# A two-layer graph network: record positions found in two parts, checks put behind the normalisation, casts split four to three

## What is computed

```python
h = relu(layernorm(x))
msg = w[:, None] * ((h @ W_i)[dst] + (h @ W_j)[src] + edge_attr @ W_e)
x = x + segment_sum(msg, dst) + h @ W_self
h = relu(layernorm(x))
def sage(h, Wl, b, Wr):
    return (segment_sum(h[src], dst) / max(count, 1)) @ Wl.T + b + h @ Wr.T
x = x + log_softmax(sage(relu(sage(h, W1l, b1, W1r)), W2l, b2, W2r))
```

## Time and profile before

| what | value |
|---|---|
| median of three runs | 1537.78 us |
| the profiled execution, its own time | 1539.19 us |
| its span | 1536.8 us |
| PE, weight load, DVE, ACT, POOL busy, share of the span | 80%, 64%, 68%, 46%, 70% |
| chain that ended last | POOL 27%, issue 10%, PE 5%, DMA 1% |
| mean granted clock of TensorE | 0.945 of full speed |
| queue of software gathers | 33552 packets, 69.34 MB |

### The profile page before, as it was taken

The page is one execution under the profiler, slowest core; times in us unless marked ns, Lnnn a source line. Parts: engine busy times, 40 slices in busy tenths (PEclk is TensorE's granted clock), DMA queues, the critical chain, the costliest instruction groups (busy, mean ns, idle before and its releaser), DMA issues. The chain is left out here.

```text
span 1536.8 us, 27420 instructions
## 1 busy us (share of the span) xinstructions
PE 1222.6 (80%) x9615; PEld 990.7 (64%) x9615; DVE 1048.8 (68%) x2116; ACT 713.3 (46%) x1202; POOL 1071.2 (70%) x1044
## 2 busy tenths in 40 slices
PE   0157888888898898888875489888989888879887
PEld 0146677677787677767653277667777666667665
DVE  7776777987888788877786255545554655656565
ACT  3323544654565546554675143433333444434344
POOL 4777777777777777776777547777773077777770
PEclk9998999999999999999999699999999999999998
DMA  7478545665666556644577457656665755665663
GB/s 241 112 174 251 156 142 172 196 193 149 191 205 183 162 157 193 193 136 121 190 224 241 112 161 197 167 170 174 173 175 144 191 171 162 178 189 164 181 172 87
DMA packets 320509, 266.98 MB, mean 174 GB/s; under 512 B 32329, under 2 KB 297956, under 8 KB 320372
## 3 DMA queue, kind: packets, MB, share of 16 engines
q1 hardware_dynamic: 272708, 189.44, 42.1%
q0 software_dynamic: 33552, 69.34, 17.1%
q10 hardware_dynamic: 14112, 6.43, 1.5%
HBM read 212.08 MB, written 53.00 MB: 172 GB/s over the span
## 5 line engine op out<-in xcount | busy, mean ns | idle before, releaser
L852 POOL DMA_INDIRECT Dt<-h_d,idx x624 | 626.2, 1004 | 199.0 <-issue 189.6
L1458 POOL DMA_INDIRECT Dg<-g_d,idx x390 | 418.7, 1074 | 205.7 <-issue 148.2
L1419 PE MATMUL pc<-Kt,hi 128*128 128x512 f32 (+1 forms) x980 | 400.4, 412 | 14.5 <-issue 5.8
L1419 PE MATMUL pc<-Kt,lo 128*128 128x512 f32 (+1 forms) x980 | 382.4, 394 | 0.0
L1352 DVE CAST Kt<-Ut 128x2048 fp32r<-128x2048 uint8 (+3 forms) x168 | 234.4, 1402 | 53.1 <-PE pc L1419 44.1
L1247 ACT ACTIVATE Cb<-pc 128x784 uint8<-128x784 f32 x304 | 240.2, 823 | 50.9 <-PE pc L1235 48.6
L1419 PEld LDWEIGHTS pc<-Kt,hi 128*128 128x128 f32 x980 | 192.4, 196 | 57.9 <-issue 17.0
L1419 PEld LDWEIGHTS pc<-Kt,lo 128*128 128x128 f32 x980 | 191.9, 196 | 34.6
L1354 ACT ACTIVATE Kt<-Ut 128x1536 fp32r<-128x1536 uint8 (+3 forms) x112 | 181.6, 1623 | 64.4 <-PE pc L1419 55.8
L1209 DVE TENSOR_TENSOR Jt<-ps,keyT 128x1568 bf16<-128x1568 bf16 x204 | 196.5, 969 | 4.5 <-PE pc L1235 1.7
L1235 PE MATMUL pc<-Jt,Rt 128*128 128x196 bf16 x1216 | 148.4, 252 | 42.6 <-ACT Cb L1247 33.9
(11 more groups left out here) (155 smaller groups left out, 1545.9 us busy)
## 6 DMA issues: line engine op xcount, KB each, us to landing
Ut<-c_d SPq DMA_DIRECT2D x126, 448.0 KB
Dt<-in_ea SPq DMA_DIRECT2D x208, 192.0 KB
c_d<-Cb SPq DMA_DIRECT2D x38, 784.0 KB
Dq<-in_ea SPq DMA_DIRECT2D x77, 192.0 KB
Dt<-h_d,idx POOLq DMA_INDIRECT x624
g_d<-ht ACTq DMA_DIRECT2D x98, 64.0 KB
r_d<-rt SPq DMA_DIRECT2D x98, 64.0 KB
sp<-g_d SPq DMA_DIRECT2D x14, 448.0 KB, 4.8
```

Of the source, the lines that this page charges most:

```text
L852: e.indirect_dma_start(Dt[:, s, t, 0:128], None, h_d, bass.IndirectOffsetOnAxis(idx[:, c:c + 1], 0))\
L1419: last = e.matmul(pc[:, k % 2, 0:n], part[:, q, :], Kt[:, t % NK, j - q0, 0:n], start=(x == 0 and t % 2 == 0 and j == 0 and part is hi), s ...
L1458: e.indirect_dma_start(Dg[:, s, t, :], None, (g1_d, g2_d)[L], bass.IndirectOffsetOnAxis(idx[:, c:c + 1], 0)).then_inc(s_gg[s], 16)
```

## The change

1. **Start.** `chk` is loaded in two pieces: the 234 columns that the window starts need go first, the 1671 columns of the checks after the seven parts of `H`. The checks (L381 to L390) and the copy of the flag run on DVE behind the last `scale`. The positions are found in two parts, windows 0 to 6 after `scale(2)` and 7 to 12 after `scale(4)`, each once its own gathers have landed, and POOL starts its window gathers with the first part.
2. **Node counts.** They are a task of their own behind `flip_weights`, with their store; `flip_counts` moves from group 1 to group 3.
3. **Weights in PSUM.** For four octets at a time DVE copies the three parts of the weights from `wp` to a corner of PSUM bank 3 (`wpp`), and the multiplications read them there. `give_r` of layer 1 moves from bank 3 to bank 2.
4. **Block normalisation.** The step that adds epsilon to the variance (L1061) goes; ACT adds it as a bias of the root, and the three Newton steps are written in another form, as many as before.
5. **Casts.** `unit_by` was: two units in five on ACT, whatever their size. Now every unit of four row blocks is on ACT, every unit of three on DVE.

```diff
+PARTS = ((0, 7), (7, NWC))
 LAG = {
-    "count.pe": 1, "load_group.sp": 5, "load_group.dve": 1,
+    "count.pe": 1, "load_group.sp": 5, "load_group.dve": 1, "flip_weights.dve": 1, "node_counts.dve": 1,
+    "node_counts.sp": 5,
 }
+        epst = sb("epst", [128, 1], F32)
+        wpp = ps[3][:, :].bitcast(BF16)[:, 512:704].rearrange("p (a w two) -> p a w two", w=32, two=2)
         def common_sp(e):
-            e.dma_start(chk[:, :], A["chk"]).then_inc(s_ld, 16)
+            e.dma_start(chk[:, KC:NCHK], A["chk"][:, KC:NCHK]).then_inc(s_ld, 16)
...
+            e.dma_start(chk[:, 0:KC], A["chk"][:, 0:KC]).then_inc(s_lk, 16)
...
+            def positions(part):
+                k0, k1 = PARTS[part]
+                n = k1 - k0
+                e.wait_ge(s_rf[part], 16 * n)
+                link(e, e.tensor_tensor(rcm[:, k0:k1, :], rows[:, k0:k1, :],
+                                        thr[:, k0:k1].unsqueeze(2).broadcast_to([128, n, 128]), ALU.is_lt))
+                link(e, e.tensor_reduce(cnt[:, k0:k1], rcm[:, k0:k1, :], AX.X, ALU.add))
...
             stats(0)
             for c in range(7):
                 if c + 1 < 7:
                     stats(c + 1)
-                if c == 1:
-                    e.wait_ge(s_vp, 1)
-                    e.tensor_copy(flag[0:1, 0:1], ps[2][0:1, 0:1]).then_inc(s_flag, 1)
                 scale(c)
-                if c == 2:
-                    e.wait_ge(s_rf, 16 * NWC)
...
+                if c in (2, 4):
+                    positions((c - 2) // 2)
+            checks()
+            e.wait_ge(s_vp, 1)
+            e.tensor_copy(flag[0:1, 0:1], ps[2][0:1, 0:1]).then_inc(s_flag, 1)
...
             for k in range(KW):
+                if k == PARTS[0][0]:
+                    e.wait_ge(s_pos, 1)
+                if k == PARTS[1][0]:
+                    e.wait_ge(s_pos, 2)
...
             e.sem_inc(s_tab, 1)
+
+        def node_counts(e):
             here = rows[:, :, :].bitcast(F32)
...
-            def shifted(e):
-                e.wait_ge(s_t3, n + 1)
                 if n >= 2:
                     e.wait_ge(s_q2, n - 1)
-                e.tensor_scalar(ve[:, i, 0:1], mv[:, i, 0, 1:2], EPS, None, ALU.add).then_inc(s_x1, 1)
+                e.bn_aggr(mv[:, i, 0, :], st[:, i, 0, :]).then_inc(s_x1, 1)
...
-                e.activation(sd[:, i, 0:1], ve[:, i, 0:1], ACT.Sqrt).then_inc(s_q2, 1)
+                e.activation(sd[:, i, 0:1], mv[:, i, 0, 1:2], ACT.Sqrt, bias=epst[:, 0:1]).then_inc(s_q2, 1)
...
-            o = (0, 3)[L]
+            o = (0, 2)[L]
...
+                    if m % 4 == 0:
+                        pair = wp[:, :, 8 * m:8 * m + 32, :].rearrange("p a w two -> p a (w two)").bitcast(F32)
+                        link(e, e.tensor_copy(ps[3][:, 256:352].rearrange("p (a w) -> p a w", w=32), pair))
                     for part, to in ((1, RW[:, m % 2, 0, :, :]), (2, RW[:, m % 2, 1, :, :]), (0, own)):
-                        e.tensor_tensor(pairs(to), pairs(own), each(wp[:, part, 8 * m:8 * m + 8, :], 64), ALU.mult)
+                        e.tensor_tensor(pairs(to), pairs(own), each(wpp[:, part, 8 * (m % 4):8 * (m % 4) + 8, :], 64), ALU.mult)
...
-        unit_by = ["act" if t % 5 in (1, 3) else "dve" for t in range(4 * NI)]
+        unit_by = [("act", "dve")[t % 2] for t in range(4 * NI)]
...
-        task("take_group", dve=windows, sp=cnt_out)
+        task("take_group", dve=windows)
...
         flip_weights()
+        task("node_counts", dve=node_counts, sp=cnt_out)
...
-                if g == 1 and u == 1:
+                if g == 3 and u == 1:
                     flip_counts()
```

More of the change, by code:

```diff
@@ L318, in build @@
         s_ld = sem("s_ld")
+        s_lk = sem("s_lk")
         s_li = sem("s_li")
@@ L322, in build @@
         s_c1 = sem("s_c1")
-        s_rf = sem("s_rf")
+        s_rf = [sem(f"s_rf{i}") for i in range(2)]
         s_pos = sem("s_pos")
@@ L380, in common_dve, with checks @@
             e.tensor_tensor(wv[:, 13:26], cnt[:, :], con[:, CC2:CC2 + NWC], ALU.is_gt)
[L381 to L390, removed]
+            def checks():
+                e.wait_ge(s_lk, 16)
+                e.scalar_tensor_tensor(wv[:, 26:29], chk[:, KL:KL + 3], -31.0, chk[:, KF:KF + 3], ALU.add, ALU.is_gt)
+                e.tensor_tensor(wv[:, 29:30], chk[:, KG:KG + 1], con[:, CLB:CLB + 1], ALU.is_lt)
+                e.tensor_tensor(wv[:, 30:31], chk[:, KH:KH + 1], con[:, CUB:CUB + 1], ALU.is_gt)
+                link(e, e.tensor_tensor(ck1[:, 0:831], chk[:, KA:KA + 831], chk[:, KA + 1:KA + 832], ALU.is_gt))
+                e.tensor_reduce(wv[:, 31:32], ck1[:, 0:831], AX.X, ALU.add)
+                e.tensor_scalar(ck2[:, 0:831], chk[:, KA:KA + 831], 2, None, ALU.arith_shift_right)
+                link(e, e.tensor_scalar(ck3[:, 0:831], chk[:, KB:KB + 831], 2, None, ALU.arith_shift_right))
+                link(e, e.tensor_tensor(ck1[:, 0:831], ck2[:, 0:831], ck3[:, 0:831], ALU.is_equal))
+                link(e, e.tensor_reduce(wv[:, 32:33], ck1[:, 0:831], AX.X, ALU.add))
+                e.tensor_reduce(vt[:, :], wv[:, 0:33], AX.X, ALU.add).then_inc(s_v, 1)
             def stats(c):
@@ L414, in scale @@
                     .then_inc(s_rs, 1)
+            def positions(part):
[5 more added lines that the diff above has]
+                link(e, e.tensor_reduce(cnt[:, k0:k1], rcm[:, k0:k1, :], AX.X, ALU.add))
+                link(e, e.scalar_tensor_tensor(c1f[:, k0:k1], c1f[:, k0:k1], 128.0, cnt[:, k0:k1], ALU.mult, ALU.add))
+                if part == 0:
+                    e.tensor_scalar(pos[:, k0:k1], c1f[:, k0:k1], 2.0, None, ALU.mult).then_inc(s_pos, 1)
+                else:
+                    e.tensor_scalar(pos[:, k0:KW], c1f[:, k0:KW], 2.0, None, ALU.mult)
+                    e.tensor_scalar(pos[:, KW:NWC], c1f[:, KW:NWC], 3.0, None, ALU.mult).then_inc(s_pos, 1)
             stats(0)
@@ L456, in common_pool @@
             e.wait_ge(s_c1, 1)
[L457 to L460, removed]
+            for part, (k0, k1) in enumerate(PARTS):
+                for k in range(k0, k1):
+                    e.indirect_dma_start(rows[:, k, :], None, A["dsr"], bass.IndirectOffsetOnAxis(c1i[:, k:k + 1], 0))\
+                        .then_inc(s_rf[part], 16)
             for k in range(KW):
+                if k == PARTS[0][0]:
+                    e.wait_ge(s_pos, 1)
+                if k == PARTS[1][0]:
+                    e.wait_ge(s_pos, 2)
                 e.indirect_dma_start(win[:, k, :], None, A["rec"], bass.IndirectOffsetOnAxis(pos[:, k:k + 1], 0))\
@@ L689, in build @@
                              "s_qe", "s_mm")]
-        s_t1, s_t2, s_t3, s_t4, s_t5, s_t6, s_t7 = [sem(f"s_t{i}") for i in range(1, 8)]
+        s_t1, s_t2, s_t4, s_t5, s_t6, s_t7 = [sem(f"s_t{i}") for i in (1, 2, 4, 5, 6, 7)]
         s_h, s_pt, s_pv, s_pr, s_pq = [sem(n) for n in ("s_h", "s_pt", "s_pv", "s_pr", "s_pq")]
@@ L1070, in act @@
                     e.wait_ge(s_r2, n - 1)
-                e.activation(sd[:, i, 0:1], ve[:, i, 0:1], ACT.Sqrt).then_inc(s_q2, 1)
-            task("block_mix", pe=pe, dve=[product, add, moments, variance, shifted], sp=[sp], act=[act])
+                if n == 0:
+                    e.wait_ge(s_ep, 1)
+                e.activation(sd[:, i, 0:1], mv[:, i, 0, 1:2], ACT.Sqrt, bias=epst[:, 0:1]).then_inc(s_q2, 1)
+            task("block_mix", pe=pe, dve=[product, add, moments, variance], sp=[sp], act=[act])
         def block_norm(b):
```

27 lines of the change are left out of this document (12 added, 15 removed).

## The result

The changed kernel takes 1499.99 us (median of 4 runs, 1498.96 to 1503.49), the kernel before 1538.59 beside it (4 runs, 1536.27 to 1540.11): a ratio of 0.9754, 95% interval 0.9733 to 0.9776. Run again later beside 11 runs of the kernel before at 1540.02, it took 1499.72, ratio 0.9733 [0.9691, 0.9776]. The profiled execution has a span of 1497.0 us, where it was 1536.8.

A forecast was written before the change was run, and what follows sets the result against it. POOL's gathers bound stage 2, PE with DVE mostly stage 1. Start and node counts +2, DVE -2, stage 1's end -1, layers -18 and -19, ACT +4: -34 us off the median 1537.8, forecast 1504, range 1491 to 1523.

The forecast's parts named there:

- What bounds which stage: Stage 2 is bound by POOL; stage 1 by PE with DVE, and by POOL only from 703 us to its end.
- The casts: Stage 2: no casts of 2048 on DVE saves POOL 40 us; -18 in layer 0, -19 in layer 1 reach the end.
- ACT, +4: Stage 2: ACT's large casts sometimes come late for PE, costing 4 us, bounds 0 and 31.
- The start: Before stage 1's gathers: POOL's first gather at 47 to 50 us, DVE's first step at 45.5 to 48.5, first `Jt` +3.
- +2, -2 and -1 for stage 1: Start and node counts +2 us, DVE in the middle of stage 1 -2, end of stage 1 -1.
- (c): Stage 1 bound by POOL, or start's gain passes through: another 8 to 20 us, 1485 to 1497; chance 0.09.
- (d): Stage 2: DVE's three-row-block casts hold POOL too, or the delay has another source: 1537 to 1541 us; chance 0.04.
- (a): ACT becomes stage 2's limit; if half the gain, 17 us, is eaten, 1521 us; chance 0.12.
- (b): Stage 2: ACT's casts so late that the kernel is slower, 1544 us at 0.35 us each; chance 0.03.

The follow-up runs named there:

- casts alone: The kernel before with only the casts split four to three between ACT and DVE: 1504.51 us, ratio 0.9759 to the kernel before.
- four outer: The changed kernel with DVE's casts written over four column parts as outer dimension instead of three row blocks: 1546.28 us, ratio 1.0038 to the kernel before.
- mixed split: The changed kernel with the old split of casts for each layer's first nine and last thirteen units: 1493.24 us, ratio 0.9706 to the kernel before.
- the repeat: The changed kernel run again unaltered, beside a kernel before of 1540 us: 1499.72 us, ratio 0.9733.

## Why the prediction was right, step by step

**What bounds which stage.** Right. Stage 2 follows POOL: 44 us less of gathers brought 35.5 (casts alone), 52.6 us more cost 46.6 (four outer). Stage 1 does not: 16 us more of POOL in it moved the time by -0.9.

**The casts.** Right in mechanism, too small in size. I charged 40 us of POOL and 37 at the end of the layers; the gathers lost 45.5, and from the first gather to PE's last full group the layers are 20.9 and 23.3 us shorter where I had 18 and 19. My count of the kernel before had put gathers that touch a cast of each size with the rest. By any overlap, 67 met casts of 2048 alone and lost 39.2 us against 0.945 each, and 17 met both sizes and lost 7.4 more; both losses went. Gathers that meet no cast took 0.952 us before and 0.956 after.

**ACT, +4.** The term was mis-sized, and I had it at another place: late ACT casts spread over the layer. PE's waits for ACT's casts came to 2.4 us at the start of the stage and 1.7 in layer 1, and two waits for DVE's casts in the middle of layer 1 to 7.3. The loss shows in the stage at its seams, 5.3 us ahead of its first gather and 6.2 behind its last. The mixed split gave back 4.4 of the first and 4.1 of the second (against the repeat). At the end the cause was not ACT's load alone, as four outer shows, but the order of DVE's slow casts and ACT's behind them. The 3.5 us that the mixed split leaves there are PE behind POOL: it starts its last full gather group 1.7 us after POOL's last gather, where it started 2.2 us ahead of it before the change. Two misses cancelled: inside the layers POOL's part became 45.1 us shorter where I had 37, and the seams cost 11.5 where I had 4. That the time came out 4 us from the forecast is in part luck.

**The start.** The forecast of 47 to 50 us for POOL's first gather failed: 44.12. I had bounded it by POOL's branch behind the flag at DVE's price of 4.46 us; the row says that it waited for `h_d`. DVE's 45.95 lay within its 45.5 to 48.5. The first `Jt` was 0.8 us later, not 3, since the weights came 4.2 us earlier. None of it matters at the end: +2, -2 and -1 for stage 1 stand against -3.1, and -2.5 in the repeat.

**The rivals.** (c) fell by the run with the weights in SBUF. (d) fell by the gathers beside the slow casts, and by four outer, which is that rival built: 1546 where I had worked out 1537 to 1541. (a) and (b) did not come: PE's waits for ACT's casts stayed at 4.1 us. The page VectorE: DVE Perf Modes of the Trainium skill (section Mode 2x_2P) grants the two-port mode to an even outermost dimension, or to an odd one that is equal on both sides. I had read the trace wrongly against this page. The source code writes three row blocks on both sides, but in a full unit the three rows of the destination touch, and the trace records the cast with three rows at the source and one run of 1536 elements at the destination. Three and 1536 are neither both even nor equal, so by the page such a cast is slow, and it took 1745 ns. Four outer is recorded with four on both sides and took 972 ns. The 14 short casts of 768 elements are recorded with three on both sides; they took 701 ns on average, and at the slow rate half the elements would have taken at least half of 1745 ns, 873 (an estimate). The trace agrees with the page in all three, and the page was no ground for (d). The forecast did not suffer, because it went by the measured durations.

## What to carry to other kernels

Where POOL issues gathers on the bound path, read each gather beside what DVE does at that moment: a fast DVE instruction can be the dearer one. Look for the same element count at two speeds, and choose the slow order where DVE has slack. Judge the shape of an access by the pattern that the trace records, not by the source, since rows that touch were recorded here as one run. And before taking load off an engine, ask whether somebody waits for it in that stage: 44 us off stage 2's gathers brought 35.5 of 40.3 us, 19 us off stage 1's only made POOL wait.

## What the runs showed of the hardware that was not expected

The first is the price of an order of visit: 972 or 1746 ns for one and the same cast of 128 x 1536 from uint8 to fp32r, written with four or three as its outer dimension, and on average 1.40 against 0.95 us for the gather beside it.

The second is open. Beside a kernel before of 2132 us the variant with four outer took 2170.43 us, later 1546.28. Its waits in both (PE's weight loads first, total, times, longest):

```profile
PEld pc L1263 <- issue: 249.2, 153, 11.5
POOL Dt L877 <- PE ps L902: 537.6, 46, 23.8
```

```profile
PEld pc L1263 <- issue: 54.4, 106, 1.2
```

Casts and gathers last as long in both (975 and 972 ns; 970 and 973 ns in stage 1), and the DMA queue with most of the traffic was busy for the same time (29.4% of 2179.8 and 41.5% of 1547.7 us, 641 and 642 us). What differs is, first, TensorE's mean granted clock, 0.81 against 0.94; PE was busy for 1397 us instead of 1230. Second, there are pauses of more than 5 us for which the profile names no instruction as releaser: 31 ahead of weight loads, 55 on DVE and 45 on ACT, against one each in the later run. PE's longer busy time accounts for 167 of the 632 us at most, and what brings the pauses stays open. In that condition all variants run were slower than the kernel before, by 1 to 3.5%; the changed kernel itself was not among them. That faster gathers buy nothing there fits POOL's waits for PE; why the variants even lose isn't shown.
